# New issue orders for the ramp, and context rows on ScalarE's DMA queue, in a fused cross-attention and quantized-FFN kernel

## What is computed

```python
mask = j_idx % n_q == i_idx                      # n_q 2048, n_kv 154
sim = where(mask, q @ k.T * scale, -max)         # so row i < 154 sees key i alone,
out = softmax(sim) @ v                           # every other row sees all keys alike
x = x + out @ Wout + bout
h = layernorm(_layernorm(x), gamma, beta)
h = gelu(qlinear(h, w1, b1))                     # 8-bit activations, ternary weights
x = x + qlinear(h, w2, b2)                       # hidden size 2048
# act_quant: scale = 127 / max|row|;  weight_quant: scale = 1 / mean|w|, w to -1, 0 or 1
```

## Time and profile before

| | us |
|---|---|
| median of 3 runs (541.22 to 542.7) | 541.96 |
| the profiled execution | 543.86 |
| its span | 542.0 |
| PE busy in it | 521.8 |
| DVE, ACT, POOL busy | 452.4, 436.8, 408.4 |

### The profile page before, as it was taken

How to read it: one execution, slowest core, us unless ns; L and a number is a source line. 1 busy time by engine, 2 the same in 40 slices (tenths; PEclk the granted TensorE clock), 3 DMA queues, 4 the chain that set the end, 5 groups by cost and what they waited for, 6 DMA issues and landing times.

```text
span 542.0 us, 8082 instructions
## 1 busy us (share of the span) xinstructions
PE 521.8 (96%) x2387; PEld 226.6 (42%) x2434; DVE 452.4 (83%) x758; ACT 436.8 (81%) x444; POOL 408.4 (75%) x533
## 2 busy tenths in 40 slices
PE   6999789799999999999999999999999999999997
PEld 3443334344444444444444444444444444444443
DVE  1799998999998888888888888889888889877653
ACT  1478988878888888888888888888888888887762
POOL 2099796988998888888898888888888889863300
PEclk8999999999999999999999999999999999999999
DMA  7996834486555545555665446556555554534433
GB/s 271 400 343 217 221 76 106 131 205 161 141 141 142 122 124 120 129 132 138 142 139 125 123 121 142 141 109 138 118 131 132 138 142 103 103 70 98 102 77 97
DMA packets 137014, 78.72 MB, mean 145 GB/s; under 512 B 114245, under 2 KB 114309, under 8 KB 136971
## 3 DMA queue, kind: packets, MB, share of 16 engines
q1 hardware_dynamic: 135819, 76.12, 55.4%
q10 hardware_dynamic: 1152, 2.10, 1.1%
HBM read 33.88 MB, written 17.05 MB: 94 GB/s over the span
## 4 chain that ended last, share of the span: by engine, by line
PE 77%; DVE 3%; issue 2%; ACT 1%; DMA 1%; DVEq 0%; ACTq 0%
PE py L1049 37%; PE p L1034 36%; PE p L1024 3%; DVE hmax L811 1%; DMA hT<-hq 1%; DVE hx L788 1%; DVE hid L805 0%; ACT hid L574 0%; ACT hq L583 0%; DVE xr L834 0%; DVE stat L780 0%; DVE xmax L793 0%; ACT hqT L592 0%; DVE hqT L825 0%; DVE hstep L814 0%
## 5 line engine op out<-in xcount | busy, mean ns | idle before, releaser
L1034 PE MATMUL p<-w1q,xqT 128*128 128x512 bf16 x995 | 229.1, 380 | 3.7 <-issue 1.6
L1049 PE MATMUL py<-w2q,hqT 128*128 128x512 bf16 x1006 | 229.9, 379 | 1.9 <-DVE hqT L825 1.0
L574 ACT ACTIVATE hid<-p,xdeq 128x1024 f32<-128x1024 f32 x128 | 141.8, 1108 | 27.1 <-PE p L1034 17.5
L583 ACT ACTIVATE hq<-hid,hscale 128x2048 int8<-128x2048 f32 x64 | 128.1, 2002 | 42.9 <-DVE hscale L817 42.9
L1049 PEld LDWEIGHTS py<-w2q,hqT 128*128 128x128 bf16 x1024 | 100.1, 98 | 122.1 <-DVE hqT L825 1.5
L1034 PEld LDWEIGHTS p<-w1q,xqT 128*128 128x128 bf16 x1024 | 94.8, 98 | 122.1 <-issue 14.3
L385 POOL TENSOR_TENSOR xr<-xr,attn 128x512 f32<-128x512 f32 x64 | 83.3, 1321 | 19.1 <-DVE attn L723 19.1
L811 DVE TENSOR_REDUCE hmax<-hid 128x1 f32<-128x1025 f32 x64 | 78.1, 1220 | 21.1 <-ACT hid L574 20.7
L400 POOL TENSOR_TENSOR hx<-hx,beta_b 128x512 f32<-128x512 f32 x64 | 91.9, 1456 | 2.0 <-ACT hx L559 2.0
L404 POOL TENSOR_TENSOR xr<-xr,b_b 128x512 f32<-128x512 f32 x64 | 93.0, 1474 | 0.0
L805 DVE TENSOR_REDUCE hid<-hid 128x1 f32<-128x1024 f32 x64 | 77.4, 1210 | 8.9 <-ACT hid L574 8.9
(11 more groups left out here) (86 smaller groups left out, 293.1 us busy)
## 6 DMA issues: line engine op xcount, KB each, us to landing
xr<-x SPq DMA_DIRECT2D x64, 256.0 KB, 2.9
out<-xr SPq DMA_DIRECT2D x64, 256.0 KB, 2.4
raw<-w1T SPq DMA_DIRECT2D x8, 512.0 KB, 11.3
wout<-wout_d ACTq DMA_DIRECT2D x8, 256.0 KB, 8.2
hid<-wvT SPq DMA_DIRECT2D x8, 256.0 KB, 10.0
wout<-w2T SPq DMA_DIRECT2D x3, 512.0 KB, 8.2
xr<-w2T SPq DMA_DIRECT2D x2, 512.0 KB, 6.4
attn<-ctxm_d SPq DMA_DIRECT2D x4, 256.0 KB, 8.5
```

What stands on the lines that cost most here:

```text
L574: nc.scalar.activation(hid[:, t % 2, h * HALF:(h + 1) * HALF], p1[:, h * HALF:(h + 1) * HALF], ACT.Gelu, scale=col(xdeq, t)).then_inc(gelu ...
L583: nc.scalar.activation(hq8[:, t % 2, :], hid[:, t % 2, 0:HID], ACT.Copy, scale=col(hscale, t))\
L1034: mm = nc.tensor.matmul(p1[:, n * D:(n + 1) * D], xT[:, k, :], w1q[:, k, n * D:(n + 1) * D], start=False, stop=(k == KD - 1))
L1049: mm = nc.tensor.matmul(py[:, t % 2, :], hqT[:, t % 2, c // 2, c % 2, :], w2q[:, c, :], start=(c == 0), stop=(c == 2 * NJ - 1))
```

## The change

The two loads of the context rows of batch 0 leave SP's queue and become the first two entries of ACT's, ahead of the chunks of Wout. On SP only the small load of b1 is ahead of the chunks of Wv; the broadcast of gamma follows them (behind x(1)), that of beta stands behind the sixth part of w1, and x(0) slips in ahead of the last chunk. The hand-written orders of all five engines are replaced and reach up to step 7; the loops begin at s = 8. No operation is added or taken away, and no size changes. The rows that a reader needs of the new orders are these:

```diff
-            load_ctx_b0()
             load_b1()
-            sp.dma_start(gamma_b[:, :], gamma.partition_broadcast(P)).then_inc(gamma_loaded, 16)
             load_wv(0)
...
             load_wv(6)
+            load_x(0)
             load_wv(7)
-            load_x(0)
...
         def _(act):
+            act.dma_start(ctx_rows, ctx_b0[0:P, :]).then_inc(ctx_b0_loaded, 16)
+            act.dma_start(ctx_end, ctx_b0[P:KV, :]).then_inc(ctx_b0_loaded, 16)
             for m in range(KI):
                 act.dma_start(wout[:, m, :], wout_d[m * P:(m + 1) * P, :]).then_inc(chunk_loaded[m], 16)
...
-            for s in range(6, T + LAG):
+            for s in range(8, T + LAG):
```

More of the change, by code:

```diff
@@ L293, in _ @@
             load_b1_rows()
+            load_x(5)
             load_w2(0)
@@ L296, in _ @@
             load_w2(1)
-            transpose_x(0)
+            load_x(6)
             load_w2(2)
             load_w2(3)
+            transpose_x(0)
             load_w2(4)
@@ L332, in _ @@
             spread_tail(1)
-            store(1)
-            for s in range(6, T + LAG + 2):
+            transpose_h(5)
+            spread_tail(2)
+            transpose_x(8)
+            transpose_h(6)
+            spread_tail(3)
+            store(0)
+            store(1)
+            load_x(16)
+            store(2)
+            store(3)
+            transpose_x(9)
+            load_x(17)
+            load_x(18)
+            for s in range(8, T + LAG + 2):
                 if s % 2 == 1:
@@ L633, in _ @@
             gelu(0, 0)
-            round_x(2)
+            times_std(4)
             gelu(0, 1)
-            round_x(3)
+            times_std(5)
             round_weights(1, 0)
             round_weights(1, 1)
-            round_x(4)
-            round_x(5)
+            round_weights(1, 2)
             gelu(1, 0)
+            times_std(6)
             gelu(1, 1)
             round_h(0)
-            round_weights(1, 2)
+            times_std(7)
+            gelu(2, 0)
+            round_x(4)
+            gelu(2, 1)
+            round_x(5)
+            round_h(1)
             round_weights(1, 3)
+            gelu(3, 0)
+            widen_h(0)
+            gelu(3, 1)
             round_weights(1, 4)
[L647 to L653, removed]
             round_weights(1, 5)
-            widen_h(0)
             round_weights(1, 6)
@@ L658, in _ @@
             round_h(2)
-            widen_h(1)
             gelu(4, 0)
+            gelu(4, 1)
+            times_std(8)
             round_x(6)
             round_x(7)
-            gelu(4, 1)
-            times_std(8)
+            widen_h(1)
+            round_h(3)
+            gelu(5, 0)
+            gelu(5, 1)
+            round_h(4)
             widen_h(2)
             times_std(9)
[L667 to L670, removed]
+            gelu(6, 0)
+            widen_h(3)
+            gelu(6, 1)
             times_std(10)
+            round_h(5)
+            widen_h(4)
+            round_x(8)
+            round_x(9)
             times_std(11)
-            widen_h(3)
-            for s in range(6, T + LAG):
+            gelu(7, 0)
+            round_h(6)
+            widen_h(5)
+            times_std(12)
+            gelu(7, 1)
+            times_std(13)
+            for s in range(8, T + LAG):
                 if live(s - 1):
@@ L887, in _ @@
             clip(0, 1)
+            statistics(6)
             clip(0, 2)
             clip(0, 3)
-            attn_rows(1)
-            attn_rows(2)
+            ctx_sum(3)
+            centre(6)
             weight_sum(1)
@@ L1070, in _ @@
             first_layer(1, 1)
-            out_rows(3)
+            tail_product()
             bias(2)
@@ L1083, in _ @@
             second_layer(0, NJ)
-            second_layer(1)
             bias(5)
             first_layer(5, 0)
-            second_layer(2)
-            first_layer(5, 1)
-            for s in range(6, T + LAG):
+            first_layer(5, 1)
+            second_layer(1)
+            bias(6)
+            first_layer(6, 0)
+            first_layer(6, 1)
+            second_layer(2)
+            bias(7)
+            second_layer(3)
+            first_layer(7, 0)
+            second_layer(4)
+            first_layer(7, 1)
+            for s in range(8, T + LAG):
                 if live(s):
```

222 lines of the change are left out of this document (119 added, 103 removed).

## The result

| | before | after |
|---|---|---|
| median of 4 runs each | 542.33 (541.22 to 543.89) | 550.21 (548.62 to 552.89) |
| ratio, 95% interval | | 1.015 [1.0121, 1.0179] |
| the profiled execution, its span | 543.86, 542.0 | 548.62, 546.8 |

The change made the kernel slower by 1.5%, where 1% faster was forecast.

The account below looks back on a forecast made before the run. PE, busy 521.8 of 542.0 us, was taken as the bound, with bias(9)'s start setting the end: 51.0 + 63.1 + 5.2 = 119.3 against 124.62, 5.3 gained, median 536.6 us; own range 534.5 to 539, 8 in 10 532.5 to 541.

Parts of the forecast that it names:

- Term 1: The start, up to the copied mean row: earlier Wv chunks bring it at 22.8 instead of 27.2, gaining 4.4 us.
- The hole: DMA engines half idle between 5 and 8 us (137 GB/s in window 5:6), taken to stay after the change.
- rival A: Start: the DMA hole between 5 and 8 us goes away, chunks come some 2.3 us sooner; 533.5 us, chance 0.18.
- rival B: Start: only bytes count, chunks come 0.65 us earlier, PE keeps its hole and low clock; 540.8 us, chance 0.08.
- Term 2: Mean row to first layer: first_layer(0) starts at 51.0 against 54.88, 3.9 us gained, bounds 48.5 and 53.
- Term 3: first_layer(0) to bias(9): 63.1 us work plus 5.2 waits, bias(9) at 119.3 against 124.62, 5.3 us gained.
- rival D: SP's ordered queue: tile 8 rows after 107.3 delay bias(9), slower than before from 113.6; 544 us, chance 0.06.
- Rival C: Hand-over: GpSimd idles five us in widen_x(6, 2) for round_x(7), most gain lost; about 540 us, chance 0.14.
- All behind bias(9) is PE-paced: Loop from step 9: PE sets the pace, so every us in bias(9)'s start is a us of the end.

Follow-up runs that it names:

- e8: Kernel before with only the context rows' loads moved to ACT's queue ahead of Wout, gamma left ahead of Wv: 539.89 us, 0.9958.
- e2: Changed kernel with spread_tail(1) ahead of transpose_h(3) on SP instead of behind transpose_h(4): 547.09 us, 1.008 against before.
- e11: e6 with round_weights(1, 3) and (1, 4) moved ahead of gelu(2, 0) on ACT: 540.29 us, 0.9974 against before.
- e1: Changed kernel with transpose_x(9) directly behind transpose_x(8) on SP: 551.19 us, 1.0167 against before.
- e3: Changed kernel with both SP edits, those of e1 and e2: 548.11 us, 1.0108 against before.
- e6: e3 with SP's stores and x loads also spread, each load some 7 us behind its store: 542.98 us, 1.0002 against before.
- e4: Kernel before with only the new start loads (context rows on ACT, gamma behind x(1)), old orders kept: 538.63 us, 0.9937.
- e5: Changed kernel with the old start loads, new orders kept: 556.45 us, 1.0262 against before.
- e10: Changed kernel with 12 and 7 useless matmuls on PE ahead of bias(8) and bias(9): 549.78 us, 1.0141 against before.
- e9: Kernel before with only gamma's load moved behind x(1): 538.2 us, 0.9944.

## Why the prediction was wrong

**Term 1 was right.** The mean row was copied at 21.68 to 22.37, forecast 22.8; PE's first product came at 6.85, forecast 7.3 to 8.0 (in the other traces with this start it came at 7.4 to 8.6). The hole was assumed to stay; it went, which was rival A's mechanism. But the mean row came only 0.4 us sooner than forecast, where the bound for that case was 2.6 more.

The Trainium skill (DMA: Bandwidth & Descriptors, section Issuing engines are not separate DMA queues) says that a second issuing engine saves sequencer time only. In e8 nothing but the queue of two loads changed, and the kernel became faster by 0.42% [0.25, 0.6], 2.3 us; the first product came at 8.21. That is more than the two issues of some 0.4 us that rival B allowed. But it isn't shown that the longer of the two queues decides: SP's first issue of Wv moved from 2.50 to 1.63 and its last from 8.1 to 5.8, since one issue had taken 2.03 us before and none took over 0.81 in e8. So time on the issuing engine can account for it as well, and the case doesn't separate the two.

**Term 2 was right, and a little low.** w1's scale at 38.1 (forecast 39.3), the first clip at 47.73 (forecast 47.7), the first layer at 49.10 (forecast 51.0).

**Term 3 was wrong, in its waits.** The step read "63.1 work + 5.2 waits". The work was right (78.6 us less waits and low clock are 63.0). The waits were 12.3, and 3.3 us of low clock came on top, for which the sum had no term: 49.1 + 63.1 + 12.3 + 3.3 = 127.8, the row says 127.74. Of the 8.4 us over the forecast of 119.3, the earlier start gave back 1.9, waits took 7.1 and the clock 3.3. Another 1.6 us of low clock stand in first_layer(9). By place:

- bias(8), 3.79 against 1.2. The step said that only gelu would be waited for. It took rows(8) to be ready at 107.3, which is where they were before the change (107.62); they were at 113.94. Ahead of them GpSimd now waited 3.67 us for round_x in widen_x(6, 2), 2.5 for statistics, and 4.83 for the rows of spread_tail(1). The last is the link that had no price: add_attention(14) ahead of tile 8 on GpSimd, and its rows behind two transposes of h on SP, each of which waits for a round_h of ACT. It could have been read in the two orders. e2 takes this wait away; the rows came 1.7 us earlier. add_attention(14) behind the rows of tile 8, as before, was not tried alone.
- bias(9), 2.04 against 0. This is rival D, with the right place and nearly the right threshold: "from 113.6 on the kernel is slower than before". Rows were ready at 113.94. From there to bias(9) the rival had 11 us; it took 13.8. The wait for store(0) was priced at 2.4, the median landing of all stores, and took 3.8: the four stores issued from 117.9 to 123.5 landed after 3.3 to 4.9 us. bias(9) came 2.4 us behind the end of the transpose's issue, where 1.5 were taken, and the issue of load_x(16) (0.34) was not counted.
- 1.09 at weight_total and 2.04 at second_layer(0) for w2q: neither was looked at; beside w1q the prediction followed only the bias rows. e11 took most of the second away.
- bias(1), 2.07 for gelu against 1.2.

**Rival D had 0.06 and should have had far more.** The prediction had the mechanism, the place and the threshold, and then held it off with one number, 107.3, walked along five queues without an error on it. Rival C's idle time of 5 us on GpSimd came too, at the place it named, with 3.67 us, and the 4.83 us came on top. C and D are one chain: what makes GpSimd late is what brings SP's order into play. They were given chances as if they were alternatives.

**"All behind bias(9) is PE-paced" was a wrong inference** from a trace in which that held, though it isn't where this forecast failed: less its 1.6 us of low clock after has 417.5 us behind bias(9), where before has 417.4. e1 and e3 show waits at bias(10) and bias(11). And "the loop's slack on the other engines is unchanged" didn't count that SP entered the loop with its stores and loads bunched. Where they were spread (e6), it is 418.2 us from bias(9) to the end, with one wait of 0.69 for gelu.

**What is shown and what is not.** That the new orders cost the time and the start loads gain some is shown (e4, e5). That SP's order from spread_tail(1) to load_x(18) is worth 8 of the 11.6 us that the orders cost under the new start loads is shown (e6 against after, 1.5%; after against e4, 2.1%); that its links hang together, by e1 and e3, where mending one link only moved the wait. Of the 3.5 us that e6 is still behind e4 by the ratios, the wait for w2q with its low clock makes 2.05 + 1.7 = 3.7 in the trace; e11 took 3.0 of these away in its trace, but only 1.5 by the ratios. In that trace 1.3 us more of waiting at weight_total (1.72 against 0.45) and 0.7 more of low clock at bias(1) took most of the rest back; it is the slowest of e11's runs, and why these two moved is open. So is why GpSimd's rows of spread_tail(1) land 5 us after SP's first issue (6.7 in e10), and how much of the 11.6 us GpSimd's own order has, with add_attention(14) ahead of tile 8.

## What to carry to other kernels

An engine that only issues DMAs is still a strictly ordered queue: before moving anything on it, write down for each entry what it waits for and who waits for the entries behind it, above all for a load that waits for the store of its own slot. Do the same for a consumer that moves up on another engine: here the loads stood where they had stood, and the add that needs them had moved ahead of other work. A hand-walked due time on which the sign of a forecast hangs needs an error of its own; here 6.6 us on 107 decided the case. And if mending one wait on such a queue gains nothing, look one and two tiles later before calling the wait free: here one mended link gave back 0.7% (e2), a second one nothing (e3), and the whole group had to be spread again (e6) before most of it came back.

## What the runs showed of the hardware beyond that

- **Short waits mostly cost more than their length.** Between 40 and 150 us PE had 22 waits of 2.04 us and more without fillers in after and in eight of the experiments. Behind 19 of them the next 16 matmuls ran at the lower level for part of their length (5.0 to 6.2 us where 3.62 is usual); behind three they did not (2.04 for w2q in after and in e1, 2.99 in e3). Not all stood alone: in seven of the eight kernels with the new orders a wait of 0.45 to 1.72 at weight_total stands just ahead of the one at bias(1). Of the ten waits of 1.59 to 1.95 in all traces one ran into a wait of 2.06 (1.72 in e11), and of the nine others one was followed by the lower level (1.90 in e8). So 2.04 us of waiting mostly cost 3.7, and the same wait for w2q, 2.04 long, cost 1.7 more in e2, e3 and e5 than in after and e1. The Trainium skill (TensorE: Matmul & The Clock Gate, section HAM oscillation) has waits for data in the middle of a kernel bringing the clock down anew each time; the rows agree for 19 of these 22.
- **A broadcast of 256 KB ahead of other loads went with a hole.** With gamma ahead of the chunks the lowest window of a microsecond between 4 and 7 us had 137 (before), 135 (e8) and 160 GB/s (e5); with it behind them none had under 258 (after, e4, e9). Its move alone was worth 3.0 us, where its bytes at 402 GB/s are 0.65. What makes the hole isn't shown.
- **The same kernel differs by its clock.** Ten runs of e2 went from 541.92 us with a mean granted clock of 1.000 to 549.67 with 0.987. A clock that is lower by 0.013 over 547.9 us is 7.1 us lost, of the 7.75 between the two. So the clock accounts for most of that spread; which waits brought it down in which run isn't shown, as each kernel has one trace.
